# A two-layer recurrence: the projections into PSUM spread over all steps, and the forget gate moved to another bank

## Chip, core and metric

One of the eight cores of a Trainium2 chip runs the kernel. The metric is the time of one execution in microseconds (us); lower is better. Engines are named as in the profile: PE (TensorE matmuls), PEld (TensorE weight loads), DVE (VectorE), ACT (ScalarE), POOL (GpSimd), SP (the queue that issues most DMAs).

## What is computed

N = 32 sequences of T = 128 steps with 128 features pass through two recurrent layers, each with a residual.

```python
def _L0_cond_ref(x, h0, Wx, Wh, b):          # layer 0, an LSTM
    xW = jnp.einsum('ntd,dg->ntg', x, Wx) + b
    def step(carry, xw_t):
        prev_h, prev_c = carry
        a = xw_t + prev_h @ Wh
        i = jax.nn.sigmoid(a[:, :Hdim])
        f = jax.nn.sigmoid(a[:, Hdim:2 * Hdim])
        o = jax.nn.sigmoid(a[:, 2 * Hdim:3 * Hdim])
        g = jnp.tanh(a[:, 3 * Hdim:])
        next_c = f * prev_c + i * g
        next_h = o * jnp.tanh(next_c)
        return ((next_h, next_c), next_h)
...
def _L1_cond_ref(x, h0, weight, bias):       # layer 1, a UGRNN
    def step(h, xt):
        m = jnp.concatenate([xt, h], axis=-1) @ weight + bias
        c = jnp.tanh(m[:, units:])
        g = jax.nn.sigmoid(m[:, :units] + 1.0)
        h_new = g * h + (1.0 - g) * c
        return (h_new, h_new)
...
x = x + _L0_cond_ref(x, cond_1024, L0_cond_Wx, L0_cond_Wh, L0_cond_b)
x = x + _L1_cond_ref(x, cond_1024, L1_cond_weight, L1_cond_bias)
```

## The kernel before

Everything lies transposed: features on the 128 partitions, the 32 sequences in the free dimension. Each engine runs its own program, a body of 16 steps (`BODY`) that is written out in full: once for the first 16 steps, six times as a hardware loop, once for the last 16. Inside a body `j` is the step, `m = j // 8` the half and `k = j % 8` the place in the half. Semaphores with the step as their count order the engines; nothing is scheduled automatically, so the order in the code is the order on each engine.

A step of layer 0 goes round a loop. PE adds `Wh` times the state to the four gate sums in PSUM: the forget gate by an fp32 matmul on `hT` (`forget_sum`, L253), the others by three bf16 matmuls on `h_high` (`high`, L259) and one fp16 matmul on `h_low` (`low`, L263). Before, `high` of i and of g come first, then `low` of i and of g, then o. ACT applies the activations, always in the order forget, i, g, o (`gates`, L436). DVE multiplies the forget gate by the old cell (`keep`, L533), makes the new cell by a scan over pairs (`scan`, L539, once into the PSUM bank `cell_bank` for ACT and once into SBUF as `cell_kept`), ACT takes its tanh (L453), and DVE makes `hT`, `h_high` and `h_low` from it (L546, L547, L553). The forget gate is written into `act_bank` at columns 0 to 31, next to the tanh of the cell at 32 to 63. Since `h_high` of the step before reads that bank, ACT waits for `high_ready` as well as for `f_summed` ahead of the forget gate.

Layer 1 runs one step behind: 8 matmuls on `h_high` and `h_low` (`layer1_input`, L271 and L273), 12 on three parts of its own state (L279: `acts`, `u_rest`, `u_low`), two tanh on ACT (L458, L459), and on DVE `pair`, the state, `u_rest`, `u_low` and the two residual sums `x1T` and `outT` (L560 to L593). On DVE these are placed between `h_high` and `scan`, and `u_low` (L577) stands between `keep` and `scan`.

The input parts, x times the input weights plus bias, don't depend on the state. They are put into PSUM ahead, each gate's bank for 8 steps at a time: `project0` issues an fp32 matmul pair of 256 columns and a bias matmul of 256 columns at the end of the step before the bank's first one. `BEGIN = (3, 4, 5, 6)` gives the place at which the banks of f, i, g and o begin, so these land at the end of the steps k = 2, 3, 4 and 5. Layer 1's part takes a 256-column pair at k = 6 and at k = 7 (`project1`, L237) and a bias matmul of 512 columns at k = 0 (`bias1`, L242). At k = 1 nothing is projected. At k = 2 of the first half the PE waits on four semaphores (three x chunks and `f_ready`) ahead of the projection.

Ahead of step 0, 11 dummy matmuls (`WARM`) run while weights and x are being loaded; then come the first projections and `first_state` of i, g and o (there is no old cell in step 0), and layer 1's first projection.

Of the kernel before, what the change touches and what calls it, by code (L numbers as in the profile page):

```python
# [10 lines left out]
P = 128  # L11
N = 32
T = 128
GS = 8
HS = 4
# [14 lines left out]
BEGIN = (3, 4, 5, 6)  # L30
# [7 lines left out]
WARM = 11  # L38


def two_layer_recurrence(nc, xt, h_first, wx, wh, b, w1, out_t):
# [5 lines left out]
    with ctx:  # L47
# [136 lines left out]
        def _(sp):  # L184
# [40 lines left out]
        def _(pe):  # L225
            def project0(q, first, steps=GS):

                k = (first - BEGIN[q]) % GS
                to = gate_banks[q][:, k * N:(k + steps) * N]
                nc.tensor.matmul(to, wx_s[:, q * P:(q + 1) * P], xT[:, first * N:(first + steps) * N],  # L230
                                 start=True, stop=False, skip_group_check=True)
                nc.tensor.matmul(to, bias_lhs[:, :], pick[:, q:q + 1].to_broadcast([P, steps * N]),
                                 start=False, stop=False, skip_group_check=True)

            def project1(q, c, first):
                weights = w1x_gate[:, :] if q == 0 else w1_raw[:, 0, P:2 * P]
                return nc.tensor.matmul(a1[c][:, :].rearrange("p (t g n) -> p t g n", t=GS, g=2)[:, :, q, :], weights,  # L237
                                        xT[:, first * N:(first + GS) * N].rearrange("p (t n) -> p t n", t=GS),
                                        start=q == 0, stop=False, skip_group_check=True)

            def bias1(c):
                nc.tensor.matmul(a1[c][:, :].rearrange("p (t g n) -> p t g n", t=GS, g=2), bias_lhs[:, :],  # L242
                                 pick[:, NG:NG + 2].unsqueeze(1).unsqueeze(3).to_broadcast([P, GS, 2, N]),
                                 start=False, stop=False, skip_group_check=True)
# [62 lines left out]
            for _ in range(WARM):  # L307
                nc.tensor.matmul(a1[1][:, 0:2 * P], idle[:, 0:P], idle[:, :], start=True, stop=True,
                                 skip_group_check=True)

            pe.wait_ge(x_in[0], 16)
# [8 lines left out]
            project0(GATE_G, 0, BEGIN[GATE_G])  # L320
            first_state(GATE_G, g_summed)
            project0(GATE_O, 0, BEGIN[GATE_O])
            first_state(GATE_O, o_summed)

            project0(GATE_F, 1, BEGIN[GATE_F] - 1)
            pe.wait_ge(w1_gate_ready, 1)
            project1(0, 0, 0)
            bias1(0)

            def body(s0, first, last):  # L330
                for j in range(BODY):
                    s, m, k = s0 + j, j // GS, j % GS
                    r, l = s - 1, (j - 1) % BODY
                    if not (first and j == 0):
# [6 lines left out]
                        high(GATE_G, j)  # L341
# [3 lines left out]
                        low(GATE_I, j, i_summed)  # L345
                        low(GATE_G, j, g_summed)
                        high(GATE_O, j)
                        low(GATE_O, j, o_summed)
                        if first and j == 1:
                            project1(1, 0, 0)  # L350
# [5 lines left out]
                        else:  # L356
                            if first and j == 2:
                                pe.wait_ge(w1_cast, 4)
                                pe.wait_ge(w1_split, 4)

                            pe.wait_ge(acts1_ready, s - 1)
# [4 lines left out]
                        if k == 0:  # L366
                            bias1(m)

                    ends = last and m == 1
                    steps = BODY - 1 - j if ends else GS  # L370
                    if k == BEGIN[GATE_F] - 1:
# [317 lines left out]
```

## Time and profile before

| | |
|---|---|
| median of 3 runs | 246.23 us (245.77 to 249.11) |
| the profiled execution, its own time | 246.65 us |
| its span from first to last instruction | 244.9 us |
| PE busy | 227.5 us (93%) |
| DVE busy | 219.7 us (90%) |
| ACT busy | 117.8 us (48%) |
| granted TensorE clock, mean | 0.931 of full speed |

The span has 128 steps in it, each of which depends on the one before, so the time is a start, 127 step lengths, and an end. The share of an engine's busy time says little here, since matmuls overlap; the spacing of the steps says more. The profiled execution took 1.75 us more than its span, and 0.42 us more than the median.

### The profile page before, as it was taken

The page shows a single profiled execution, that of the slowest core. Times are in us where ns is not written, and L with a number is a line of the kernel's source. Part 1 is how long each engine was busy: PE and PEld are TensorE (multiplying, and loading weights), DVE is VectorE, ACT ScalarE, POOL GpSimd, SP SyncE. Part 2 cuts the span into 40 slices and gives each one's busy share as a digit, 9 for nine tenths or more (in the row PEclk, how much of TensorE's full clock was granted, in tenths as well). Part 3 has the DMA queues.
Part 4 walks back from the last instruction along what each step waited for, and adds up shares of the span by engine and source line. Part 5 has one row for each costly group of instructions (what it writes and reads, how often), then busy time and mean ns, then how long its engine had stood idle before and what let it go on. Part 6 is the DMA issues. An engine that isn't in the chain of part 4 may idle for free.

```text
span 244.9 us, 12629 instructions
## 1 busy us (share of the span) xinstructions
PE 227.5 (93%) x4631; PEld 193.3 (79%) x4631; DVE 219.7 (90%) x1557; ACT 117.8 (48%) x906; POOL 4.0 (2%) x12
## 2 busy tenths in 40 slices
PE   6999898999989899998989989898999989899993
PEld 4888787878878787887878778787878878787882
DVE  6669999999988989999997989999999999979884
ACT  3445455554544445454553544545554554545441
POOL 1400000000000000000000000000000000000000
PEclk9999999999989979999997979999999999979655
DMA  6000001000010000100010000100001000000000
GB/s 184 12 4 25 24 23 37 25 25 19 19 43 11 21 21 21 32 21 21 11 43 21 11 21 21 32 21 21 21 22 31 21 21 21 12 15 13 15 13 11
DMA packets 11969, 6.20 MB, mean 25 GB/s; under 512 B 1446, under 2 KB 11692, under 8 KB 11948
## 3 DMA queue, kind: packets, MB, share of 16 engines
q1 hardware_dynamic: 11792, 5.66, 8.1%
q8 instruction: 13, 0.21, 0.4%
q10 hardware_dynamic: 156, 0.27, 0.3%
q14 instruction: 8, 0.07, 0.1%
HBM read 3.82 MB, written 2.10 MB: 24 GB/s over the span
## 4 chain that ended last, share of the span: by engine, by line
DVE 61%; PE 21%; ACT 9%; issue 5%; DMA 1%; SPq 0%; ACTq 0%
DVE cell_bank L539 11%; ACT act_bank L453 8%; DVE hT L546 8%; DVE u_low L577 7%; DVE pair L560 6%; DVE u_rest L572 5%; DVE acts L566 5%; PE gate_f L253 4%; DVE x1T L585 4%; DVE h_high L547 4%; PE gate_f L230 4%; DVE outT L593 4%; DVE h_low L553 4%; PE a L279 3%; DVE scan_add L533 3%
## 5 line engine op out<-in xcount | busy, mean ns | idle before, releaser
L253 PEld LDWEIGHTS gate_f<-hT,wh_raw 128*128 128x128 f32 x254 | 42.1, 207 | 38.4 <-DVE hT L546 34.5
L436 ACT ACTIVATE act_bank<-gate_f 128x32 f32<-128x32 f32 x127 | 23.1, 182 | 79.6 <-PE gate_f L253 79.6
L253 PE MATMUL gate_f<-hT,wh_raw 128*128 128x32 f32 x254 | 51.1, 285 | 10.7 <-DVE hT L546 10.7
L271 PE MATMUL a<-h_high,w1x_part 128*128 128x32 f16 x768 | 42.1, 178 | 0.9 <-DVE h_low L553 0.9
L453 ACT ACTIVATE act_bank<-cell_bank 128x32 f32<-128x32 f32 x128 | 23.3, 182 | 36.7 <-DVE cell_bank L539 36.6
L539 DVE TENSOR_TENSOR_SCAN cell_bank<-scan_mul,scan_add 128x64 f32<-128x64 f32 x128 | 38.6, 301 | 1.1 <-ACT scan_add L436 1.1
L279 PE MATMUL a<-acts,w1h_part 128*128 128x32 bf16 x762 | 38.6, 178 | 0.0
L273 PE MATMUL a<-h_low,w1x_fp 128*128 128x32 f16 x256 | 35.7, 178 | 0.0
L539 DVE TENSOR_TENSOR_SCAN cell_kept<-scan_mul,scan_add 128x64 f32<-128x64 f32 x128 | 34.2, 267 | 0.0
L546 DVE TENSOR_TENSOR hT<-out_gate,act_bank 128x32 f32<-128x32 f32 x128 | 23.8, 186 | 10.5 <-ACT act_bank L453 1.2
L271 PEld LDWEIGHTS a<-h_high,w1x_part 128*128 128x128 bf16 x768 | 31.9, 97 | 1.3 <-ACT acts L459 0.9
L259 PEld LDWEIGHTS gate_i<-h_high,wh_part 128*128 128x128 bf16 x381 | 32.3, 132 | 0.0
L279 PE MATMUL a<-u_rest,w1h_part 128*128 128x32 bf16 x508 | 32.2, 178 | 0.0
L533 DVE TENSOR_TENSOR scan_add<-act_bank,cell_kept 128x32 f32<-128x32 f32 x127 | 24.3, 191 | 7.7 <-ACT act_bank L436 7.2
L560 DVE SCALAR_TENSOR_TENSOR pair<-acts 128x64 f32<-128x64 f32 x128 | 28.7, 224 | 1.4 <-ACT acts L459 1.4
L259 PE MATMUL gate_i<-h_high,wh_part 128*128 128x32 f16 x381 | 29.9, 180 | 0.0
L458 ACT ACTIVATE acts<-a 128x64 f32<-128x64 f32 x128 | 28.1, 219 | 1.9 <-PE a L279 1.5
L259 PE MATMUL gate_g<-h_high,wh_part 128*128 128x32 f16 x381 | 29.0, 178 | 0.0
L259 PE MATMUL gate_o<-h_high,wh_part 128*128 128x32 f16 x381 | 29.0, 178 | 0.0
L279 PEld LDWEIGHTS a<-acts,w1h_part 128*128 128x128 bf16 x762 | 28.3, 97 | 0.0
L279 PE MATMUL a<-u_low,w1h_part 128*128 128x32 bf16 x254 | 27.6, 185 | 0.0
L436 ACT ACTIVATE out_gate<-gate_o 128x32 f32<-128x32 f32 x128 | 26.3, 205 | 1.1 <-PE gate_o L248 1.1
(97 smaller groups left out, 612.8 us busy)
## 6 DMA issues: line engine op xcount, KB each, us to landing
xT<-in_x_dram SPq DMA_DIRECT2D x46, 64.0 KB, 1.8
out_dram<-outT SPq DMA_DIRECT2D x32, 64.0 KB, 1.6
wx_s<-in_L_cond_Wx_dram SPq DMA_DIRECT2D x1, 256.0 KB, 2.7
wh_raw<-in_L_cond_Wh_dram ACTq DMA_DIRECT2D x1, 256.0 KB, 2.9
w_raw<-in_L_cond_weight_dram SPq DMA_DIRECT2D x1, 256.0 KB, 3.5
bias_rows<-in_biases_dram ACTq DMA_DIRECT2D x1, 3.0 KB
condT<-in_cond_dram SPq DMA_DIRECT2D x1, 16.0 KB, 2.5
```

Of the source, the lines that this page charges most:

```text
L253: nc.tensor.matmul(gate_step(GATE_F, j), wh_raw[:, GATE_F * P:(GATE_F + 1) * P], hT[:, (j - 1) % RING, :], start=False, stop=True, skip_gr ...
L259: nc.tensor.matmul(gate_step(q, j), wh_part[:, w, (q - 1) * P:q * P], h_high[:, (j - 1) % PARTS, :], start=False, stop=False, skip_group_c ...
L271: nc.tensor.matmul(to, w1x_part[:, w, q * P:(q + 1) * P], h_high[:, j % PARTS, :], start=False, stop=False, skip_group_check=True)
L273: nc.tensor.matmul(to, w1x_fp16[:, q * P:(q + 1) * P], h_low[:, j % PARTS, :], start=False, stop=False, skip_group_check=True)
L279: mm = nc.tensor.matmul(a1_step(j)[:, q * N:(q + 1) * N], w1h_part[:, w, q * P:(q + 1) * P], moving, start=False, stop=parts == 1, skip_gr ...
L436: return nc.scalar.activation(out, gate_step(q, j), func)
L453: nc.scalar.activation(tanh_c[:, :], cell[:, :, 1], ACT.Tanh).then_inc(tanh_c_ready, 1)
L458: nc.scalar.activation(acts1[:, 0:4:3, i, :], a1_step(j).rearrange("p (g n) -> p g n", g=2), ACT.Tanh)
L533: nc.vector.tensor_tensor(scan_add[:, :, 1], forget[:, :], cell_kept[:, :, 1], ALU.mult).then_inc(scan_in_ready, 1)
L539: nc.vector.tensor_tensor_scan(to[:, :, :].rearrange("p n two -> p (n two)"), scan_mul[:, :, :].rearrange("p n two -> p (n two)"), scan_ad ...
L546: nc.vector.tensor_tensor(hT[:, j % RING, :], out_gate[:, :], tanh_c[:, :], ALU.mult).then_inc(h_ready, 1)
L560: nc.vector.scalar_tensor_tensor(out=pair1[:, :, :], in0=acts1[:, 0:2, i, :], scalar=1.0, in1=acts1[:, 2:4, i, :], op0=ALU.add, op1=ALU.mu ...
```

## The change

Six things are changed.

1. The banks begin at other places: `BEGIN = (7, 1, 3, 5)` for f, i, g, o. Each gate's bank is filled in halves over two steps: at the first (k = 0, 2, 4, 6 for i, g, o, f) an fp32 pair of 128 columns, which opens the bank, and the bias for all 8 steps; at the second (k = 1, 3, 5, 7) the other 128-column pair.
2. Layer 1's projection is made in quarters of 128 columns, at k = 1, 3, 5 and 7; its bias goes in halves of 256 columns to k = 2 and 6. So each step of the eight now ends in some projection. Each of the two steps that fill a bank has a wait of its own for the gate having been read.
3. In the last half body, where projections shrink or fall away, 2, 2, 4, 2 and 4 dummy matmuls of 256 columns are added at k = 1, 3, 5, 6 and 7.
4. `low` of gate i is issued right behind `high` of gate i, ahead of gate g.
5. The forget gate is written into `cell_bank` (columns 64 to 95), and ACT's wait for `high_ready` is gone.
6. At the start, x chunk 0 is loaded ahead of the first state and layer 1's weights ahead of x chunk 1; gates i, g, o, f are projected for 1, 3, 5 and 6 steps; i's and g's first states are both issued ahead of o's projection; layer 1's first projection has 128 columns, and the rest of it and its bias move into the steps 1 to 3. There are 12 dummy matmuls in place of 11.

The core of the diff:

```diff
-BEGIN = (3, 4, 5, 6)
+BEGIN = (7, 1, 3, 5)
-        forget, tanh_c = act_bank[:, 0:N], act_bank[:, N:2 * N]
+        forget, tanh_c = cell_bank[:, 2 * N:3 * N], act_bank[:, 0:N]
...
             sp.dma_start(wx_s[:, :], wx).then_inc(wx_in, 16)
+            load_x(0, 0)
             sp.dma_start(condT[:, :], h_first).then_inc(cond_in, 16)
-            load_x(0, 0)
+            sp.dma_start(w1_raw[:, :, :], w1.rearrange("(h k) n -> k h n", h=2)).then_inc(w1_in, 16)
             load_x(1, 1)
-            sp.dma_start(w1_raw[:, :, :], w1.rearrange("(h k) n -> k h n", h=2)).then_inc(w1_in, 16)
...
-            project0(GATE_I, 0, BEGIN[GATE_I])
+            project0(GATE_I, 0, 1)
+            bias0(GATE_I, 0, 1)
+            project0(GATE_G, 0, 3)
+            bias0(GATE_G, 0, 3)
             pe.wait_ge(wh_in, 16)
             pe.wait_ge(cond_in, 16)
             first_state(GATE_I, i_summed)
+            first_state(GATE_G, g_summed)
             pe.wait_ge(x_in[1], 16)
...
                         high(GATE_I, j)
-                        high(GATE_G, j)
...
                         low(GATE_I, j, i_summed)
+                        high(GATE_G, j)
                         low(GATE_G, j, g_summed)
...
-                    if k == BEGIN[GATE_I] - 1:
-                        pe.wait_ge(scan_in_ready, 2 * s + 1)
-                        project0(GATE_I, j + 1, steps)
...
+                    if k == 0:
+                        if m == 0:
+                            pe.wait_ge(x_in[0], s0 + 16)
+                            pe.wait_ge(x_in[1], s0 + 16)
                         pe.wait_ge(scan_in_ready, 2 * s + 1)
+                        project0(GATE_I, a, a_steps)
+                        bias0(GATE_I, a, BODY - a if ends else GS)
+                    if k == 1:
+                        if not ends:
+                            pe.wait_ge(x_in[2 if m == 0 else 4], s0 + 16)
+                        pe.wait_ge(scan_in_ready, 2 * s + 1)
+                        project0(GATE_I, b, b_steps, False)
+                        if not ends:
+                            project1(0, 1 - m, 0, next1)
+                        else:
+                            warm(0, 2)
...
-
-                    act.wait_ge(high_ready, s)
                     act.wait_ge(f_summed, s)
```

How this moves instructions is seen at three places. The first is PE in the loop body, from the end of step j = 1 of the first half (place k = 1) into the next step. `a_0` and `a_1` are layer 1's two banks. Before:

```order
L279 MATMUL a_0<-u_low,w1h_part 128x32 [waits u_low_ready]
L279 MATMUL a_0<-u_low,w1h_part 128x32
L335 REGISTER_ALU
L253 MATMUL gate_f<-hT,wh_raw 128x32 [waits h_ready]
L259 MATMUL gate_i<-h_high,wh_part 128x32 [waits high_ready]
L259 MATMUL gate_i<-h_high,wh_part 128x32 x2
L259 MATMUL gate_g<-h_high,wh_part 128x32 x3
L263 MATMUL gate_i<-h_low,wh_fp 128x32 [waits low_ready]
L263 MATMUL gate_g<-h_low,wh_fp 128x32
```

And in the changed kernel:

```order
L287 MATMUL a_0<-u_low,w1h_part 128x32 [waits u_low_ready]
L287 MATMUL a_0<-u_low,w1h_part 128x32
L400 ISA [waits x_in2]
L229 MATMUL gate_i<-xT,wx_s 128x128 [waits scan_in_ready]
L245 MATMUL a_1<-xT,w1x_gate 128x4x32
L349 REGISTER_ALU
L261 MATMUL gate_f<-hT,wh_raw 128x32 [waits h_ready]
L267 MATMUL gate_i<-h_high,wh_part 128x32 [waits high_ready]
L267 MATMUL gate_i<-h_high,wh_part 128x32 x2
L271 MATMUL gate_i<-h_low,wh_fp 128x32 [waits low_ready]
L267 MATMUL gate_g<-h_high,wh_part 128x32 x3
L271 MATMUL gate_g<-h_low,wh_fp 128x32
```

Two 128-column pairs and two waits have come between the last matmul of layer 1 and the forget sum, where there was nothing, and gate g's three `h_high` matmuls now stand behind gate i's last.

The second place is ACT, one regular step from the forget gate to the tanh of the cell. Before:

```order
L436 ACTIVATE act_bank<-gate_f 128x32 [waits f_summed,high_ready]
L436 ACTIVATE scan_mul<-gate_i 128x32 [waits i_summed]
L436 ACTIVATE scan_add<-gate_g 128x32 [waits g_summed]
L436 ACTIVATE out_gate<-gate_o 128x32 [waits o_summed]
L453 ACTIVATE act_bank<-cell_bank 128x32 [waits cell_ready]
```

And in the changed kernel:

```order
L491 ACTIVATE cell_bank<-gate_f 128x32 [waits f_summed]
L491 ACTIVATE scan_mul<-gate_i 128x32 [waits i_summed]
L491 ACTIVATE scan_add<-gate_g 128x32 [waits g_summed]
L491 ACTIVATE out_gate<-gate_o 128x32 [waits o_summed]
L506 ACTIVATE act_bank<-cell_bank 128x32 [waits cell_ready]
```

The order is the same; the forget gate has one wait in place of two and another bank as its target.

The third place is PE at the start, from the first projection to layer 1's. Before:

```order
L230 MATMUL gate_i<-xT,wx_s 128x128 [waits pick_ready,bias_ready,wx_in,x_in0]
L232 MATMUL gate_i<-pick,bias_lhs 128x128
L248 MATMUL gate_i<-condT,wh_raw 128x32 [waits cond_in,wh_in]
L230 MATMUL gate_g<-xT,wx_s 128x160 [waits x_in1]
L232 MATMUL gate_g<-pick,bias_lhs 128x160
L248 MATMUL gate_g<-condT,wh_raw 128x32
L230 MATMUL gate_o<-xT,wx_s 128x192
L232 MATMUL gate_o<-pick,bias_lhs 128x192
L248 MATMUL gate_o<-condT,wh_raw 128x32
L230 MATMUL gate_f<-xT,wx_s 128x64
L232 MATMUL gate_f<-pick,bias_lhs 128x64
L237 MATMUL a_0<-xT,w1x_gate 128x8x32 [waits w1_gate_ready]
```

And in the changed kernel:

```order
L229 MATMUL gate_i<-xT,wx_s 128x32 [waits pick_ready,bias_ready,wx_in,x_in0]
L235 MATMUL gate_i<-pick,bias_lhs 128x32
L229 MATMUL gate_g<-xT,wx_s 128x96
L235 MATMUL gate_g<-pick,bias_lhs 128x96
L256 MATMUL gate_i<-condT,wh_raw 128x32 [waits cond_in,wh_in]
L256 MATMUL gate_g<-condT,wh_raw 128x32
L229 MATMUL gate_o<-xT,wx_s 128x160 [waits x_in1]
L235 MATMUL gate_o<-pick,bias_lhs 128x160
L256 MATMUL gate_o<-condT,wh_raw 128x32
L229 MATMUL gate_f<-xT,wx_s 128x192
L235 MATMUL gate_f<-pick,bias_lhs 128x192
L245 MATMUL a_0<-xT,w1x_gate 128x4x32 [waits w1_gate_ready]
```

Gate g's projection now stands ahead of gate i's first state and no longer waits for x chunk 1. Behind these rows the bias of layer 1 (512 columns) stood before; now a projection of gate i with its bias stands there.

## Rows read from the trace of the kernel before

**Rows 1.** The page: busy time and share by engine, and the granted clock in 40 slices.
```profile
PE 227.5 (93%) x4631; PEld 193.3 (79%) x4631; DVE 219.7 (90%) x1557; ACT 117.8 (48%) x906; POOL 4.0 (2%) x12
PEclk9999999999989979999997979999999999979655
```

**Rows 2.** Stretches between starts of `hT`: length, DVE busy on L546 (count), clock, DMA.
```profile
17.33:240.03 222.70, 23.09 (x125) 0.94 0.08 22
45.21:67.75 22.54, 2.42 (x13) 1.00 0.08 23
39.86:67.75 27.89, 2.98 (x16) 1.00 0.09 26
67.75:97.75 30.00, 2.98 (x16) 0.89 0.08 22
211.23:240.03 28.80, 2.81 (x16) 0.74 0.05 14
```

**Rows 3.** Two pairs of steps: length, busy PE, PEld, DVE, ACT, POOL, clock, DMA.
```profile
67.75:71.22 3.47, 2.70 (x70) 2.48 (x70) 3.32 (x25) 1.77 (x16) 0.00 (x0) 1.00 0.16 46
71.22:76.02 4.80, 4.80 (x76) 4.03 (x77) 3.40 (x25) 1.79 (x16) 0.00 (x0) 0.64 0.10 27
```

**Rows 4.** One regular step in order of time: start, duration, engine, line, operation.
```profile
40.10 0.41 PE L253 MATMUL gate_f<-hT,wh_raw 128*128 128x32 f32 x2 [0.23 <-DVE hT L546]
40.22 0.18 DVE L553 SCALAR_TENSOR_TENSOR h_low<-hT,h_high 128x32 f16<-128x32 f32 x1
...
40.50 0.18 PE L263 MATMUL gate_i<-h_low,wh_fp 128*128 128x32 f16 x1
...
40.61 0.18 ACT L436 ACTIVATE act_bank<-gate_f 128x32 f32<-128x32 f32 x1 [0.56 <-PE gate_f L253]
...
40.67 0.18 DVE L593 SCALAR_TENSOR_TENSOR outT<-acts,x1T 128x32 f32<-128x32 f32 x1
...
40.81 0.19 ACT L436 ACTIVATE scan_add<-gate_g 128x32 f32<-128x32 f32 x1
40.82 0.19 DVE L533 TENSOR_TENSOR scan_add<-act_bank,cell_kept 128x32 f32<-128x32 f32 x1
...
40.93 0.18 DVE L577 TENSOR_TENSOR u_low<-u_rest 128x32 bf16<-128x32 f32 x1
...
41.05 0.30 DVE L539 TENSOR_TENSOR_SCAN cell_bank<-scan_mul,scan_add 128x64 f32<-128x64 f32 x1
...
41.17 0.21 PE L279 MATMUL a<-u_low,w1h_part 128*128 128x32 bf16 x2
...
41.38 0.18 ACT L453 ACTIVATE act_bank<-cell_bank 128x32 f32<-128x32 f32 x1 [0.29 <-DVE cell_bank L539]
...
41.84 0.30 PE L253 MATMUL gate_f<-hT,wh_raw 128*128 128x32 f32 x1 [0.45 <-DVE hT L546]
```

**Rows 5.** PE at the projection of gate f, k = 2, first half of a body, full clock.
```profile
42.90 0.21 PE L279 MATMUL a<-u_low,w1h_part 128*128 128x32 bf16 x2
43.21 0.67 PE L230 MATMUL gate_f<-xT,wx_s 128*128 128x256 f32 x2
```

**Rows 6.** The same place in the second half of the body, full clock.
```profile
56.92 0.22 PE L279 MATMUL a<-u_low,w1h_part 128*128 128x32 bf16 x2
57.03 0.67 PE L230 MATMUL gate_f<-xT,wx_s 128*128 128x256 f32 x2
57.53 0.27 PE L232 MATMUL gate_f<-pick,bias_lhs 128*128 128x256 bf16 x1
57.64 0.36 PE L253 MATMUL gate_f<-hT,wh_raw 128*128 128x32 f32 x2
```

**Rows 7.** PE in the start, before the first forget sum.
```profile
8.66 1.20 PE L237 MATMUL a<-xT,w1x_gate 128*128 128x256 f32 x2
9.65 0.63 PE L242 MATMUL a<-pick,bias_lhs 128*128 128x512 bf16 x1
10.08 0.47 PE L253 MATMUL gate_f<-hT,wh_raw 128*128 128x32 f32 x2
```

More of the change, by code:

```diff
@@ L225, in _, with project0 @@
         def _(pe):
-            def project0(q, first, steps=GS):
+            def project0(q, first, steps, begins=True):
                 k = (first - BEGIN[q]) % GS
[L229 to L232, printed above, removed]
+                nc.tensor.matmul(gate_banks[q][:, k * N:(k + steps) * N], wx_s[:, q * P:(q + 1) * P],
+                                 xT[:, first * N:(first + steps) * N], start=begins, stop=False,
+                                 skip_group_check=True)
@@ L233, in project0, with bias0, half1 @@
+            def bias0(q, first, steps=GS):
+                k = (first - BEGIN[q]) % GS
+                nc.tensor.matmul(gate_banks[q][:, k * N:(k + steps) * N], bias_lhs[:, :],
+                                 pick[:, q:q + 1].to_broadcast([P, steps * N]),
                                  start=False, stop=False, skip_group_check=True)
-            def project1(q, c, first):
+            def half1(c, half):
+                return a1[c][:, half * GS * N:(half + 1) * GS * N].rearrange("p (t g n) -> p t g n", t=HS, g=2)
@@ L236, in project1 @@
+            def project1(q, c, half, first):
                 weights = w1x_gate[:, :] if q == 0 else w1_raw[:, 0, P:2 * P]
[L237 to L243, printed above, removed]
+                return nc.tensor.matmul(half1(c, half)[:, :, q, :], weights,
+                                        xT[:, first * N:(first + HS) * N].rearrange("p (t n) -> p t n", t=HS),
+                                        start=q == 0 and half == 0, stop=False, skip_group_check=True)
@@ L244, in bias1 @@
+            def bias1(c, half):
+                nc.tensor.matmul(half1(c, half), bias_lhs[:, :],
+                                 pick[:, NG:NG + 2].unsqueeze(1).unsqueeze(3).to_broadcast([P, HS, 2, N]),
                                  start=False, stop=False, skip_group_check=True)
@@ L306, in _, with warm @@
             idle = ident[:, :].bitcast(BF16)
-            for _ in range(WARM):
-                nc.tensor.matmul(a1[1][:, 0:2 * P], idle[:, 0:P], idle[:, :], start=True, stop=True,
-                                 skip_group_check=True)
+            def warm(c, times):
+                for _ in range(times):
+                    nc.tensor.matmul(a1[c][:, 0:2 * P], idle[:, 0:P], idle[:, :], start=True, stop=True,
+                                     skip_group_check=True)
+            warm(1, WARM)
             pe.wait_ge(x_in[0], 16)
@@ L356, in body @@
                         else:
+                            pe.wait_ge(acts1_ready, s - 1)
                             if first and j == 2:
+                                project1(0, 0, 1, HS)
+                                bias1(0, 1)
                                 pe.wait_ge(w1_cast, 4)
                                 pe.wait_ge(w1_split, 4)
-                            pe.wait_ge(acts1_ready, s - 1)
+                            if first and j == 3:
+                                project1(1, 0, 1, HS)
                             layer1_input(l)
```

77 lines of the change are left out of this document (50 added, 27 removed).

## The prediction

> **What bounds the kernel now.** I read the page first, then stretches cut at the starts of `hT`, then one regular step. On the page PE and DVE are both busy nearly all the time, which decides nothing, but the clock row is not even: it dips in several slices and is low for the whole end [rows 1]. The stretches turn this into step lengths. Undisturbed, 13 steps take 22.54 us, 1.734 each; a whole body of 16 steps at full clock takes 27.89, which is 16 x 1.734 = 27.74 and 0.15 more; the body at 67.75 takes 30.00 at 0.89 of the clock, and the last 15 steps 28.80 at 0.74 [rows 2]. From 17.33 to 240.03 there are 124 step lengths in 222.70 us, where 124 x 1.734 would be 215.0 [rows 2]. So 7.7 us of the span are steps longer than the regular one. Ahead lie the start (17.3 us, three long steps in it), behind the end (4.9 us).
>
> What makes the regular step 1.734 us is seen in its rows [rows 4]. The forget sum ends at 40.10 + 0.41 = 40.51, ACT starts the forget gate at 40.61, `keep` starts at 40.82, `u_low` 0.11 later, the scan at 41.05, the tanh at 41.38, and the next forget sum starts at 41.84. DVE is nearly full, but one of its starts waits: `outT` starts at 40.67 and `keep` 0.15 later, where `u_low` follows `keep` after 0.11 and `scan` follows `u_low` after 0.12. `keep` waits for the forget gate, which ends at 40.79. PE has room: between layer 1's last matmuls (41.17) and the next forget sum (41.84) lie 0.67 us [rows 4].
>
> What makes the long steps is PE's clock. At the steps k = 0 and 1, PE does little besides the recurrence: busy 2.70 of 3.47 us at full clock. The two steps behind them, which carry the large projections, then took 4.80 us at a mean clock of 0.64 [rows 3], where two regular ones take 3.47. PE's clock has fallen from 2.4 to 1.2 GHz for most of them, and at half rate a projection no longer fits into the 0.67 us.
>
> **Part 1, the projections spread out.** The same columns are projected in the loop, so the sum of PE's work stays; each step now carries two 128-column pairs, or one pair and 256 to 512 bias columns. What it removes is the pair of light steps. Of the 7.7 us, 7 bodies have the 0.15 at k = 2 (1.05 us, below), and the rest, 6.7, goes with the low clock: the body at 67.75 has 30.00 - 27.89 = 2.1 more than an undisturbed one, the body at 125.64 nearly the same (29.82 us long, 1.9), and the last 15 steps have 28.80 - 26.01 - 0.15 = 2.6 [rows 2]. Every fall of the clock in the trace stands at or just behind a pair k = 0, 1; with no light pair left I take it that the clock stays at 2.4 GHz from the third or fourth step on. The last eight steps would be light, and there the added dummy matmuls stand for the missing projections. The gain is 6.7 us; the bounds are 0 (the clock falls as often as before) and 6.7.
>
> Does a step's projection fit into the gap? A 256-column pair and its bias matmul take from 57.03 to 57.64, 0.61 us, and start 0.11 behind layer 1's last matmuls; the forget sum then starts 0.72 after them in place of 0.67 [rows 6], and the step lengths there stay regular. A 128-column pair lies between a 32-column pair (the forget sum itself, at most 0.41) and the 256-column one (0.50 to its bias matmul [rows 6]); by its columns it takes 0.25 to 0.30. Two pairs take 0.5 to 0.6, a pair with 512 bias columns 0.5: inside. The 0.15 at k = 2 of the first half: there the projection starts 0.31 behind layer 1's last matmuls [rows 5], in the second half 0.11 [rows 6]. Four semaphores are waited for in the one, two in the other. In the changed kernel no place has four; k = 0 has three, with a pair and 256 bias columns behind (0.31 + 0.30 + 0.11 = 0.72, just inside), k = 1 two, with two pairs (0.2 + 0.6 = 0.8 at worst, 0.1 late in 8 steps). I take the 1.05 us as gained and up to 0.8 as a risk.
>
> **Part 2, the forget gate.** ACT starts the tanh 0.03 behind the end of the scan (41.05 + 0.30 = 41.35, start 41.38), but the forget gate 0.10 behind its sum (40.51, start 40.61) [rows 4]. The forget gate waits for two semaphores, and `high_ready` is long there; I read the 0.06 to 0.07 as the second wait being taken up only after the first. With one wait the gate starts at about 40.55 and ends at 40.73, `keep` could start at 40.76, and DVE itself is free for it at 40.67 + 0.11 = 40.78. So `keep` gains 0.037. The other bank costs nothing: ACT and DVE touch `cell_bank` at other times. The stall goes to DVE's own order; next late is gate g.
>
> **Part 3, gate i first.** `low` of i needs `h_low`, which ends at 40.22 + 0.18 = 40.40; PE starts its matmuls 0.06 behind a DVE result (`u_low` ends at 41.11, start 41.17), so i's `low` can start between 40.46 and 40.48 (now 40.50). Three matmuls of g and its `low` follow at 0.025 each (23 matmuls lie between 40.50 and 41.17, at most 0.029 each, and the last waits), so g's sum ends at up to 40.58 + 0.18 = 40.76. ACT takes g at 40.79 where it now does at 40.81, it ends at 40.99, and the scan can start at 41.02 in place of 41.05 [rows 4]. So of the 0.037 that part 2 gives, 0.027 arrive. Over 124 steps: 3.3 us. The bounds are 0 (the two waits cost nothing, or g comes as late as now) and 4.6 (all of 0.037). I take 3.3, since each latency in it has a row of the same step.
>
> **Part 4, the start.** The first projections are narrower and layer 1's is smaller ahead of the first forget sum. The clock is low here, though the page's row doesn't show it: a 256-column pair takes 0.99 us, twice the 0.50 of later, and 512 bias columns take 0.43, with the forget sum behind them at 10.08 [rows 6, 7]. Ahead of the first `hT`, gates i, g and o lose 96 + 64 + 32 columns, 0.0039 each (0.99 / 256), 0.7 us, and a DMA is moved ahead. But what is taken out comes back between the recurrence's own matmuls: counted up to the forget sum of step 3, PE has 64 projection columns more (0.25 us) and 448 bias columns more (0.38), in four more pairs, since the new banks open earlier. The first `hT` is then 0.6 earlier, and the fourth about 0.7 later if the clock rises where it does now, or 0.7 earlier if the denser work makes it rise sooner. I take 0 with bounds of -0.8 and +0.8. The end stays: it is a chain of DVE and ACT with a store.
>
> **The sum.** Against the profiled execution: 244.9 - 6.7 - 1.05 - 3.3 + 0 = 233.9 us of span, plus the 1.75 around it: 235.6 us. That execution was 0.42 above the median of 246.23, so the ratio is about 0.956.
>
> **The rule that speaks against it.** As the trace has it, PE had no gap of its own in the pair of steps before the fall: 2.70 of 3.47 us busy [rows 3], as in the same steps of bodies in which the clock stayed. The Trainium skill, "TensorE: Matmul & The Clock Gate", section "Why this matters for your kernels", asks for no idle gaps between bursts of matmuls to keep the fast clock; by that rule alone there is nothing here for spreading to remove, and the time would be that of the rival "clock not in our hands" below. Its section "A second HAM failure mode" tells of an oscillation by small idles between groups, which is nearer to what these rows show.
>
> **Rivals.**
> 1. *The step doesn't shorten.* The scan comes no earlier, since gate g's sum comes later by the three matmuls put ahead of it, or the second wait costs nothing. For: g is behind i by four matmuls now; against: the 0.10 and the 0.03 in one step. Then 235.6 + 3.3 = 238.9.
> 2. *The clock still falls at some places.* In the last eight steps the projections with their dummies are lighter than in the loop (at k = 3 and 4 above all), and the start is another phase. A pair of steps at low clock cost 4.80 - 3.47 = 1.3 with the large projections [rows 3]; one to three of them give 237 to 239.5.
> 3. *The clock is not in our hands.* The falls have another cause than the light pairs, and come as before: 235.6 + 6.7 = 242.3. Against: all stand behind the same pair.
> 4. *PE sets the step, and the kernel is slower.* A fp32 pair could cost by instruction and not by column: then a 128-column pair takes the 0.50 of the 256-column one, two of them with the lead of 0.11 take 1.11, against 0.72 that fits. Four of eight steps (k = 1, 3, 5, 7), 60 in all, would be 0.39 longer: 235.6 + 23 = 259. It decides from 0.61 for the two pairs. Against: 256 columns at low clock take twice the time at full clock (0.99 and 0.50 [rows 6, 7]), so columns count.
>
> **How the numbers follow.** Forecast 0.62 (233 to 238), rival 1 0.16, rival 2 0.14, rival 3 0.05, rival 4 0.03. The low end is 235.6 - 1.3 (all of 0.037) - 0.8 (start) - 0.7: 232.8; the high end takes in rivals 1 and 2 and a start 0.8 longer: 240.0. Outside stay rivals 3 and 4 and edges of the rest. Two per cent, about what a measurement of this kernel can tell from no change, is at 241.3: faster 0.91, same 0.06, slower 0.03.
>
> **What would show it.** Right: a clock of 1.00 in every body and to the end; 16 steps in 27.3 us; the forget gate 0.03 to 0.04 behind its sum; `keep` 0.11 to 0.12 behind `outT`; no longer step at k = 2. Wrong: stretches of 0.5 clock in the loop (rivals 2, 3), a step of still 1.73 with gate g's activation ending later (rival 1), the forget sum idle-free behind the projections (rival 4), a fourth `hT` later than 18 us (part 4).

## The result, and the profile after

The changed kernel takes 234.18 us (median of 4 runs, 234.11 to 234.33), the kernel before beside it 247.3 us (245.77 to 249.11, 4 runs; one more than in the table ahead). The ratio is 0.947, with a 95% interval of 0.939 to 0.954. The profiled executions took 234.23 us (span 232.7) and 246.65 us (span 244.9), so 12.4 us are to be placed.

The page of the changed kernel, its busy times and its clock row; they answer to [rows 1].
```profile
PE 226.2 (97%) x4850; PEld 202.6 (87%) x4850; DVE 216.3 (93%) x1557; ACT 124.8 (54%) x906; POOL 4.0 (2%) x12
PEclk9999999999999999999999999999999999999999
```
The dips and the low end are gone. (The row reads 9 in the start too, where the matmuls run at half speed, as is seen below.) PE's busy time hardly changes (227.5 to 226.2 us), though it has 219 more matmuls to do.

Stretches between starts of `hT` (now L599), with the columns of [rows 2]: from the fifth `hT` to the last, the bodies from 37.67 and from 65.08, and the last 15 steps. The counts take in the instruction at either edge.
```profile
17.12:227.77 210.65, 23.25 (x124) 1.00 0.08 23
37.67:65.08 27.41, 3.02 (x17) 1.00 0.10 26
65.08:92.48 27.40, 3.02 (x17) 1.00 0.08 24
202.08:227.77 25.69, 2.84 (x16) 1.00 0.06 16
```
123 steps in 210.65 us are 1.7126 each, and all of them lie between 1.711 and 1.715: every body is 16 times that. In the trace the low clock is found before 10.13 us and after 232.0 only.

All engines in the pairs k = 0, 1 and k = 2, 3 of the body at 65.08, the columns of [rows 3].
```profile
65.08:68.50 3.42, 3.42 (x78) 3.24 (x79) 3.27 (x24) 1.88 (x16) 0.00 (x0) 1.00 0.16 46
68.50:71.93 3.43, 3.43 (x79) 3.09 (x76) 3.28 (x25) 1.89 (x16) 0.00 (x0) 1.00 0.06 19
```
PE is busy 3.42 us of the pair that had 2.70 of 3.47 before [rows 3]; the four steps are alike.

One regular step of the changed kernel in order of time, as in [rows 4].
```profile
39.76 0.28 PE L261 MATMUL gate_f<-hT,wh_raw 128*128 128x32 f32 x1
39.99 0.19 PE L271 MATMUL gate_i<-h_low,wh_fp 128*128 128x32 f16 x1
40.03 0.23 PE L267 MATMUL gate_g<-h_high,wh_part 128*128 128x32 f16 x3
40.08 0.18 ACT L491 ACTIVATE cell_bank<-gate_f 128x32 f32<-128x32 f32 x1 [0.50 <-PE gate_f L261]
40.11 0.18 PE L271 MATMUL gate_g<-h_low,wh_fp 128*128 128x32 f16 x1
...
40.20 0.18 DVE L646 SCALAR_TENSOR_TENSOR outT<-acts,x1T 128x32 f32<-128x32 f32 x1
...
40.30 0.18 DVE L586 TENSOR_TENSOR scan_add<-cell_bank,cell_kept 128x32 f32<-128x32 f32 x1
...
40.32 0.20 ACT L491 ACTIVATE scan_add<-gate_g 128x32 f32<-128x32 f32 x1
...
40.41 0.18 DVE L630 TENSOR_TENSOR u_low<-u_rest 128x32 bf16<-128x32 f32 x1
...
40.55 0.30 DVE L592 TENSOR_TENSOR_SCAN cell_bank<-scan_mul,scan_add 128x64 f32<-128x64 f32 x1
```
The forget gate starts 0.04 us behind its sum (39.76 + 0.28 = 40.04, start 40.08), where it was 0.10 [rows 4]. `keep` follows `outT` after 0.10 and not 0.15, `u_low` follows `keep` after 0.11. The wait stands in another place now: the scan starts 0.14 behind `u_low`, and 0.03 behind the end of gate g's activation (40.32 + 0.20 = 40.52).

PE at a step that has two projection pairs, k = 3. [rows 5, 6] show a projection in the kernel before.
```profile
42.40 0.20 PE L287 MATMUL a<-u_low,w1h_part 128*128 128x32 bf16 x2
42.45 0.48 PE L229 MATMUL gate_g<-xT,wx_s 128*128 128x128 f32 x2
42.76 0.39 PE L245 MATMUL a<-xT,w1x_gate 128*128 128x128 f32 x2
43.06 0.30 PE L261 MATMUL gate_f<-hT,wh_raw 128*128 128x32 f32 x1
```
The first pair starts 0.05 us behind the first of layer 1's last two matmuls, the second 0.31 behind the first, and the forget sum at its usual place: two pairs fit, and no step is longer at k = 2 or anywhere else.

PE in the start, which answers to [rows 7].
```profile
2.77 1.49 PE L318 MATMUL a<-ident 128*128 128x256 bf16 x6
4.05 0.61 PE L229 MATMUL gate_i<-xT,wx_s 128*128 128x32 f32 x2
...
8.08 0.69 PE L245 MATMUL a<-xT,w1x_gate 128*128 128x128 f32 x2
8.56 0.63 PE L229 MATMUL gate_i<-xT,wx_s 128*128 128x128 f32 x2
8.99 0.42 PE L235 MATMUL gate_i<-pick,bias_lhs 128*128 128x256 bf16 x1
9.20 0.47 PE L261 MATMUL gate_f<-hT,wh_raw 128*128 128x32 f32 x2
...
10.28 0.27 PE L250 MATMUL a<-pick,bias_lhs 128*128 128x256 bf16 x1
```
The same 256 bias columns take 0.42 us at 8.99 and 0.27 at 10.28: the clock has gone from 1.2 to 2.4 GHz between them. The clock events of the trace put the rise at 10.13 us, before at 16.67. And the first forget sum starts 0.88 us earlier (9.20 for 10.08 [rows 7]). The first five `hT` start at 8.08, 11.07, 13.26, 15.15 and 17.12 us; before at 9.06, 12.05, 14.75, 17.33 and 19.06. Of the 1.94 us at the fifth, 0.98 are there at the first, with the clock low in both kernels; the rest comes in the four steps behind it, in which the clock rises.

So the 12.4 us are: the bumps at k = 2 1.05; the regular step 1.7335 to 1.7126, 0.021 x 123 = 2.6; the start up to the fifth `hT` 1.94; and the low clock in the loop 6.7, which is what remains of the 10.3 us between the fifth and the last `hT`. The end stays at 4.9, and 0.15 lie outside the span.

### The profile page after: what moved, and what is told of

Its sections match the earlier page's. It is cut to its first block, busy times and chain, and to the rows that moved or that the text cites. A ratio compares the mean times of both kernels' runs of the same rounds, so it can differ in the third digit from the quotient of the medians.

```text
span 232.7 us, 12952 instructions
## 1 busy us (share of the span) xinstructions
PE 226.2 (97%) x4850; PEld 202.6 (87%) x4850; DVE 216.3 (93%) x1557; ACT 124.8 (54%) x906; POOL 4.0 (2%) x12
## 4 chain that ended last, share of the span: by engine, by line
DVE 78%; ACT 10%; PE 6%; issue 4%; POOL 0%; ACTq 0%; POOLq 0%
DVE cell_bank L592 15%; ACT act_bank L506 10%; DVE hT L599 10%; DVE u_low L630 9%; DVE pair L613 9%; DVE u_rest L625 7%; DVE acts L619 6%; DVE x1T L638 6%; DVE h_low L606 5%; DVE h_high L600 5%; DVE outT L646 5%; DVE scan_add L586 1%; PE a L318 1%; PE a L245 1%; PE a L287 1%
## 5 line engine op out<-in xcount | busy, mean ns | idle before, releaser
L491 ACT ACTIVATE cell_bank<-gate_f 128x32 f32<-128x32 f32 x127 | 23.1, 182 | 63.6 <-PE gate_f L261 63.6
L261 PEld LDWEIGHTS gate_f<-hT,wh_raw 128*128 128x128 f32 x254 | 38.0, 189 | 21.3 <-DVE hT L599 14.8
L599 DVE TENSOR_TENSOR hT<-out_gate,act_bank 128x32 f32<-128x32 f32 x128 | 24.2, 189 | 10.4 <-ACT act_bank L506 1.1
L267 PEld LDWEIGHTS gate_i<-h_high,wh_part 128*128 128x128 bf16 x381 | 30.1, 125 | 0.0
L267 PE MATMUL gate_i<-h_high,wh_part 128*128 128x32 f16 x381 | 29.3, 178 | 0.0
L491 ACT ACTIVATE scan_mul<-gate_i 128x32 f32<-128x32 f32 x128 | 25.7, 201 | 1.0 <-PE gate_i L256 0.8
L512 ACT ACTIVATE acts<-a 128x32 f32<-128x32 f32 x128 | 26.0, 203 | 0.0
L491 ACT ACTIVATE scan_add<-gate_g 128x32 f32<-128x32 f32 x128 | 25.8, 202 | 0.2 <-PE gate_g L256 0.2
```

Of the source, the lines that this page charges most:

```text
L261: nc.tensor.matmul(gate_step(GATE_F, j), wh_raw[:, GATE_F * P:(GATE_F + 1) * P], hT[:, (j - 1) % RING, :], start=False, stop=True, skip_gr ...
L267: nc.tensor.matmul(gate_step(q, j), wh_part[:, w, (q - 1) * P:q * P], h_high[:, (j - 1) % PARTS, :], start=False, stop=False, skip_group_c ...
L491: return nc.scalar.activation(out, gate_step(q, j), func)
L512: nc.scalar.activation(acts1[:, 1, i, :], a1_step(j)[:, 0:N], ACT.Tanh, scale=-1.0).then_inc(acts1_ready, 1)
L599: nc.vector.tensor_tensor(hT[:, j % RING, :], out_gate[:, :], tanh_c[:, :], ALU.mult).then_inc(h_ready, 1)
```

## The experiments

Twelve kernels, in three groups of four, each group timed beside the kernel before (medians of 245.72, 247.38 and 246.98 us). Times are medians of 4 runs. Where kernels of different groups are set beside each other, the step lengths in their traces say more than the medians. No kernel leaves out a part of the reference's computation; where dummies change, they are matmuls whose result nothing reads.

**Is it the second wait or the bank, and what does the order bring?** In the changed kernel:
```
a2   if not first:
+        act.wait_ge(high_ready, s)
         act.wait_ge(f_summed, s)
a1   high(GATE_I, j)
+    high(GATE_G, j)
     ...
     low(GATE_I, j, i_summed)
-    high(GATE_G, j)
c2   both
```
The second wait back:

> The changed kernel with ACT's wait for high_ready put back ahead of the forget gate, which still goes to cell_bank. The semaphore is long there, so only the taking up of a second wait is added. If that costs 0.06 us per step at the forget gate (my theory), the gate starts 0.10 behind its sum, keep 0.15 behind outT, the step is 1.73 and the time about 237. If the bank is what helps, the step stays 1.713 and the time 234.2.

The order back:

> The changed kernel with gate g's three h_high matmuls put back ahead of gate i's last matmul. If gate g's sum sets the scan (my theory), undoing it makes i come later and g follow it on ACT by 0.09: a step of 1.71 to 1.72 us, a time of 234.2 to 235.2. If the order is what shortens the step at all, the step is 1.73 and the time 236.5 to 237. If the order only delays g, the step is 1.70 and the time 232 to 232.8.

Both back, which leaves the spread projections and the new start:

> The changed kernel with both of its step edits undone (ScalarE's second wait and the order of the kernel before); its spread projections, its start and its dummies at the end stay. Theory, the step is then the one of before and the parts add up: a step of 1.7335 us, no clock falls before the end, no bump at k = 2; a fifth hT at 16.5 to 17.3 us, 123 steps and 4.9 us of end give a span of 234.6 to 235.5 us, total 236.4 to 237.3 us; ratio 0.955 to 0.965. Rival, the spread projections themselves lengthen or shorten the step (their places differ per step): a step off 1.7335 us by over 0.005, or unequal steps.

237.21 us (ratio 0.970, 0.963 to 0.976), 235.45 us (0.960, 0.957 to 0.963) and 236.81 us (0.961, 0.958 to 0.965). A body at full clock of each, with the columns of [rows 2] but all of DVE as the engine: with the wait back,
```profile
65.25:93.03 27.78, 26.61 (x192) 1.00 0.08 24
```
with the order back,
```profile
64.62:92.22 27.60, 26.43 (x192) 1.00 0.08 24
```
and with both back.
```profile
64.90:92.67 27.77, 26.60 (x192) 1.00 0.08 24
```
The steps are 1.736, 1.725 and 1.736 us, beside 1.7125 with neither. With the wait back, and with both back, the theories held; with the order back the step (forecast 1.71 to 1.72) and the time (up to 235.2) lie just above their theory's range. The new order brings nothing while there are two waits, and 0.0125 with one; taking the wait away brings 0.011 in the old order and 0.0235 in the new one. So each of two things sets the scan once the other is out of the way. The rows with the wait back:
```profile
48.14 0.41 PE L261 MATMUL gate_f<-hT,wh_raw 128*128 128x32 f32 x2
...
48.64 0.18 ACT L491 ACTIVATE cell_bank<-gate_f 128x32 f32<-128x32 f32 x1 [0.56 <-PE gate_f L261]
...
48.83 0.20 ACT L491 ACTIVATE scan_add<-gate_g 128x32 f32<-128x32 f32 x1
48.85 0.19 DVE L587 TENSOR_TENSOR scan_add<-cell_bank,cell_kept 128x32 f32<-128x32 f32 x1
```
and with the order back.
```profile
48.32 0.20 ACT L491 ACTIVATE scan_add<-gate_g 128x32 f32<-128x32 f32 x1
48.40 0.18 DVE L630 TENSOR_TENSOR u_low<-u_rest 128x32 bf16<-128x32 f32 x1
...
48.55 0.30 DVE L592 TENSOR_TENSOR_SCAN cell_bank<-scan_mul,scan_add 128x64 f32<-128x64 f32 x1
```
With two waits, in the cell's bank, the forget gate is again 0.09 behind its sum (48.14 + 0.41 = 48.55, start 48.64), and `keep` starts 0.03 behind the gate's end (48.82): the wait costs it, not the bank. With one wait and the old order, the scan follows 0.03 behind the end of gate g's activation (48.52): g's sum is next late. With both back the step is 1.736 for 1.7335, so the spread projections leave it as it was, to 0.003 us.

The same in the kernel before, where only the bank and the wait are changed:

> Of the whole change the kernel before gets the forget gate's move alone: it lies in the cell's bank and ScalarE waits for f's sum only. The profiled run with the second wait put back in the changed kernel had steps of 1.736 us, against 1.7125 us. If the wait alone is what those 0.023 us are, they need both parts here too: with g's high products still ahead of i's low ones, the run with the order put back gave 1.725 us. So here a regular step of 1.722 to 1.728 instead of 1.7335, which is 0.7 to 1.4 us of 124 steps; the bumps at k = 2 and the clock's falls stay as before, so 243.5 to 245.5 us in all, ratio 0.990 to 0.998. Rival, the path runs through the scan's other operand even in this order: a step of 1.733 and a ratio of 1.000. Rival, the wait is worth the same wherever the order stands: 1.710 and a ratio of 0.988.

241.29 us (0.976, 0.965 to 0.988), a step of 1.7225. A body at full clock, with its bump of 1.838 at k = 2, all of DVE:
```profile
98.64:126.31 27.67, 26.49 (x193) 1.00 0.08 24
```
The step is the first theory's. The total fell by 6 us, and not by the 0.7 to 1.4 of the expectation: the step gives 0.011 x 124 = 1.4, and the bump at k = 2 is smaller (1.830 to 1.838 us for 1.887, 0.3 in all). The rest goes with the clock. Its mean over an execution is 0.944, 0.962, 0.965 and 0.971 here, and 0.918 to 0.947 in the seven of the kernel before beside them. The trace is that of the longest of the four (245.19 us; the others took 239.3 to 242.0); the clock falls four times in its loop, where the trace of before has five falls. Why there are fewer falls with a step 0.011 us shorter stays open.

**Are the light steps what brings the clock down?** In the kernel before:
```
a4  +if k == 1:
    +    for _ in range(4):
    +        nc.tensor.matmul(a1[1 - m][:, 0:2 * P], idle[:, 0:P], idle[:, :], start=True, stop=True,
    +                         skip_group_check=True)
```


> The kernel before with four dummy matmuls of 256 columns at the end of each step k = 1 (which has no projection), nothing moved. If the light pair k = 0, 1 brings the clock down (my theory), no fall is left up to the last body, the bodies at 67.75 and 125.64 take 27.9 us, and the time is 4 us under that of before, about 242; the end stays low. If the falls have another cause, the time is that of before, 246 to 248.

239.88 us (0.977, 0.969 to 0.984). The clock row, and PE in a pair k = 0, 1 and in a body:
```profile
PEclk9999999999999999999999999999999999999995
```
```profile
66.85:70.32 3.47, 3.14 (x74) 1.00 0.16 46
...
38.92:66.85 27.93, 27.37 (x587) 1.00 0.09 26
```
Work that nothing needs, four matmuls of 256 columns in eight steps, takes the clock's falls away: PE is busy 3.14 of the pair's 3.47 us where it was 2.70 [rows 3], and the clock stays up until 232.6 us. Nothing else was moved, and the mean clock is 0.984 to 0.990 in all four executions, 0.911 to 0.951 in the seven of before. The expectation had the end staying low and 242 us; the last body has these dummies too, and its clock stayed up. The bump of 0.15 stays in six bodies; in the last it is 0.06.

In the changed kernel, without its dummies in the last eight steps:

> The changed kernel without the dummy matmuls of the last half body. If light steps bring the clock down (my theory), it is at 0.5 in part of the last eight steps and the time is 0.5 to 2 us longer, 234.7 to 236.2. If the falls have another cause, nothing changes: 234.2.

234.0 us (0.953, 0.950 to 0.956), where the changed kernel, in another group, took 234.18. The clock did fall without the dummies, at 225.43 us and so 2.7 us ahead of the last `hT` (mean clock 0.980 to 0.984 in all four executions, 0.997 to 0.999 with them), but one step of 1.911 us is all that came of it; the expectation of 0.5 to 2 us was too high.

**Is the bump at k = 2 four waits in a row?** In the kernel before:
```
b4  +if k == 1 and m == 0:
    +    pe.wait_ge(x_in[0], s0 + 16)
    +    pe.wait_ge(x_in[1], s0 + 16)
     if k == BEGIN[GATE_F] - 1:
    -    for chunk in (range(3) if m == 0 else range(4, 5)):
    +    for chunk in (range(2, 3) if m == 0 else range(4, 5)):
```


> The kernel before, where at k = 2 of a body's first half PE waits for three chunks of x ahead of gate f's projection; here two of the three waits stand at k = 1 and one stays. If the three waits in a row make the step of 1.887 us in each body (0.154 us over the regular one), it goes and each body that has a full clock lasts 27.74 us instead of 27.89: 7 x 0.15 = 1.05 us less, ratio 0.995 to 0.996. If the bump is gate f's projection landing in that step, it stays at 27.89 and the ratio is 1.000. If the waits only move, the bump comes at k = 1 instead and the body stays 27.89 us.

243.41 us (0.986, 0.976 to 0.996). A body at full clock, all of DVE:
```profile
40.70:68.44 27.74, 26.58 (x192) 1.00 0.10 27
```
27.74 for 27.89 [rows 2], and all sixteen steps between 1.733 and 1.738: the waits made the bump. At k = 1 of the loop's bodies the two that were moved cost nothing that the step lengths show; no projection stands behind them there. In the last body a step there is 1.797, 0.06 longer, which a4 has at k = 2. The total fell by 4 us, where the expectation had 1.05 (a ratio of 0.995 to 0.996); as with b1, the mean clock was higher than beside it (0.943 to 0.958 for 0.918 to 0.947), and why stays open.

**What made the start shorter?** In the changed kernel, the old order of the loads (`condT`, chunk 0, chunk 1, `w1_raw`), once with 11 dummies and once with 16:
```
b2   sp.dma_start(wx_s[:, :], wx).then_inc(wx_in, 16)
    -load_x(0, 0)
     sp.dma_start(condT[:, :], h_first).then_inc(cond_in, 16)
    +load_x(0, 0)
    +load_x(1, 1)
     sp.dma_start(w1_raw[:, :, :], ...).then_inc(w1_in, 16)
    -load_x(1, 1)
    -WARM = 12
    +WARM = 11        (c1: 16)
```


> The changed kernel with the loads issued in the order of before (h_first ahead of the first chunk, w1 behind the second) and 11 dummies instead of 12; its shorter first projections stay. The changed kernel's first five hT start at 8.08, 11.07, 13.26, 15.15 and 17.12 us and its clock rises at 10.13 us; before they start 0.98 us later at the first and 1.94 us later at the fifth, and the clock rises at 16.67 us. If the load order makes the difference, the first hT goes back by about 1 us and the total by 1 to 2 us, to 235.2 to 236.2 us. If the shorter projections in front of the first state make it (their PE time is on the path, at a clock of 1.2 GHz), the first hT stays within 0.3 us of 8.08 and the total at 234.0 to 234.6 us. The steps stay at 1.7125 us in both.

> The kernel with the old order of loads (235.5 us; x's first chunk arrives 0.74 us after the last of 11 dummies, the clock rises at 15.9 us, first hT at 8.84, fifth at 19.48 us), now with 16 dummies, which last until about 4.93 us. If TensorE's idle gap between the dummies and the first projection is what put off the clock's rise, the gap is gone and the clock rises between 4.5 and 11 us: the fifth hT at 17.0 to 18.0 us, total 233.9 to 234.7 us. Rival, only the late arrival of the chunk counts: fifth hT at 19.4 to 19.6 us and 235.3 to 235.8 us in all, as with 11 dummies.

235.54 us with 11 (0.954, 0.944 to 0.965; runs from 234.5 to 236.5) and 233.53 us with 16 (0.947, 0.944 to 0.951). PE's start with 11 dummies:
```profile
2.77 1.27 PE L318 MATMUL a<-ident 128*128 128x256 bf16 x5
4.79 0.63 PE L229 MATMUL gate_i<-xT,wx_s 128*128 128x32 f32 x2 [0.74 <-DMA xT<-in_x_dram]
...
14.68 0.42 PE L250 MATMUL a<-pick,bias_lhs 128*128 128x256 bf16 x1
```
and with 16.
```profile
2.77 2.34 PE L318 MATMUL a<-ident 128*128 128x256 bf16 x10
4.91 0.48 PE L229 MATMUL gate_i<-xT,wx_s 128*128 128x32 f32 x2
...
7.77 0.27 PE L235 MATMUL gate_i<-pick,bias_lhs 128*128 128x256 bf16 x1
```
With 11, PE is idle 0.74 us in front of its first projection; 256 bias columns still take 0.42 us at 14.68, the clock rises at 15.9 us, and the fifth `hT` starts at 19.48, as before (19.06), though the narrow projections are there. With 16 the first projection starts later still, at 4.91, but without a gap: the same columns take 0.27 us at 7.77, the clock rises at 5.67 us, and the fifth `hT` starts at 16.58, which is earlier than its theory had it (17.0 to 18.0). So the late load costs its time only where PE goes idle over it. The five dummies close the gap and are more work at once; the two are not told apart. Of all fourteen traces, the nine without a gap in front of the first projection have the clock up from between 4.2 and 5.7 us on (six of them) or from 10.1 to 10.4 us (three), the five with one (0.54 to 1.47 us) from between 10.8 and 21.3 us on, the earliest of them with a gap of 0.85. What decides between the early and the late ones of a kind stays open. The Trainium skill, "TensorE: Matmul & The Clock Gate", section "Why this matters for your kernels", asks for TensorE to be kept busy continuously to get its full clock; here, in the start, the trace agrees (a gap of 0.74 us and the rise at 15.9, none and the rise at 5.67).

**Can gate g come earlier still?** In the changed kernel one (b3) or two (c3) of g's three high products stand ahead of i's `low`:
```
b3   high(GATE_I, j)
    +high(GATE_G, j, range(1))            (c3: range(2))
     ...
     low(GATE_I, j, i_summed)
    -high(GATE_G, j)
    +high(GATE_G, j, range(1, 3))         (c3: range(2, 3))
```


> The changed kernel with the first of gate g's three high products issued ahead of gate i's low ones, and two behind them. Of the changed kernel's step i's sum is done 0.10 us ahead of g's, and ScalarE does i first anyway; with all three of g's ahead the step is 1.725 us. If PE only fills a gap there (it waits for u's low half at that place), the first product costs i's sum nothing and brings g's sum forward by one matmul of about 0.025 us: a step of 1.69 to 1.705 us, 1 to 2.5 us less in all, 231.7 to 233.2 us. If PE is never idle between them, i comes later by as much as g is earlier by nothing: 1.7125 us or up to 1.717 us, 234.2 to 234.8 us.

> With one of gate g's high products ahead of i's low one the step is 1.700 us; here two are ahead. In that trace TensorE has a gap of one product's time (0.604 minus 0.567 us, against 0.025 us of one) in front of i's low product, and one after it; ScalarE works i, g, o at 0.094 and 0.082 us behind one another, i first. Theory, i's sum now sets ScalarE's chain: a second product ahead moves i's low product by 0.01 to 0.025 us, so the step is 1.708 to 1.725 us, 233.0 to 235.0 us in all. Rival, g's sum still sets it: the step falls by another 0.013 us to 1.687, 230.4 us in all.

232.02 us with one (0.942, 0.933 to 0.951) and 232.37 us with two (0.942, 0.938 to 0.946); the step is 1.700 in both. PE and ACT with one ahead:
```profile
47.56 0.18 PE L267 MATMUL gate_g<-h_high,wh_part 128*128 128x32 f16 x1
47.60 0.19 PE L271 MATMUL gate_i<-h_low,wh_fp 128*128 128x32 f16 x1
...
47.83 0.20 ACT L492 ACTIVATE scan_mul<-gate_i 128x32 f32<-128x32 f32 x1
...
47.92 0.20 ACT L492 ACTIVATE scan_add<-gate_g 128x32 f32<-128x32 f32 x1
```
and with two.
```profile
48.22 0.18 PE L271 MATMUL gate_i<-h_low,wh_fp 128*128 128x32 f16 x1
...
48.44 0.20 ACT L492 ACTIVATE scan_mul<-gate_i 128x32 f32<-128x32 f32 x1
...
48.53 0.20 ACT L492 ACTIVATE scan_add<-gate_g 128x32 f32<-128x32 f32 x1
```
One product ahead is free: PE waits for `h_low` there. The second brought neither what its theory said nor its rival: i's `low` starts 0.013 later but takes 0.177 in place of 0.189 us, so its sum is done at the same 0.79 us behind `hT`, ACT starts i at 0.83 and g 0.094 behind it in both. (The profile models the ends of matmuls; that ACT starts at the same time is measured.) From here on, by these rows, gate i's sum and ACT's spacing set the scan; the row of g's sum (done 0.03 us earlier with two) has no say.

**Does it take the spread projections at all?** The kernel before with five small edits: the dummies of a4, the bank and the wait of b1, the waits of b4, the order of b3, and the changed kernel's order of loads with 12 dummies (all shown above).

> The kernel before with its projections where they were, and five small edits: four dummies of 256 columns at each k = 1 (239.9 us), forget gate beside the cell with one wait, one of g's high products ahead of i's low ones, two of the x waits at k = 1, the new order of loads with 12 dummies. If the parts add up whatever carries them: the clock up throughout, a step of 1.700 us, bodies of 27.2 us without a bump, fifth hT at about 17.5 us, 232.0 to 233.5 us in all. Rival, the lumps of projection (512 columns in one step) meet the shorter step: a bump of 0.05 us or more at k = 2, 3, 4 or 5 of each half, 16 x 0.05 to 0.15 = 0.8 to 2.4 us more, 233.5 to 236 us.

232.37 us (0.944, 0.940 to 0.949). PE from the fifth `hT` to the last, and in one body:
```profile
16.60:225.74 209.14, 204.07 (x4503) 1.00 0.08 24
64.21:91.41 27.20, 26.68 (x586) 1.00 0.08 24
```
16 steps in 27.20 us, without a bump: the parts add up, whatever carries them. The start too: with the wide first projections of before, its fifth `hT` starts at 16.60, as with the narrow ones and 16 dummies (16.58; the clock rises at 5.05 and 5.67), so the loads and the dummies make the start, and the narrow projections are not needed for it. This kernel is as fast as the one with spread projections and the same order (232.02), and both are faster than the changed kernel (234.18, in another group) by some 2 us, 0.0125 x 123 = 1.5 of it by the step.

## Why the prediction was right, and where not

The forecast was 235.6 us and a ratio of 0.956, measured were 234.2 and 0.947. Point by point:

**Clock and spreading (part 1): right in mechanism and size.** 6.7 us of falls are gone. That light steps bring the clock down was an inference from where the falls stood; dummies at k = 1 alone showed it. The objection that PE had "no gap of its own" there was read too coarsely: in such a pair PE is idle in spells of 0.23 and 0.45 us [rows 4], none in the loop is longer than 0.45, and bodies with a fall and without one have the same. The dummies fill the spell of 0.45 and add work at once, and the falls are gone; the two are not told apart. A 128-column pair was put at 0.25 to 0.30 us and takes 0.31 from its start to the next one's. The 1.05 us of the bumps is right to 0.1 (the last body's is 0.06, where it can be seen), and so is the cause, with the waits split. The 0.8 us of risk at k = 1 did not come. That the last eight steps need their dummies was so for the clock and not for the time.

**Forget gate (part 2): right.** The gate starts 0.04 behind its sum, `keep` 0.10 behind `outT` (forecast 0.11 to 0.12).

**Gate i first (part 3): right mechanism, 0.7 us too large.** The forecast was 0.027 us of a step and 3.3 in all, measured were 0.021 and 2.6. Counted from `hT`, i's `low` starts at 0.604 us (forecast 0.60 to 0.62), g's at 0.718 (0.72), ACT's g at 0.931 (0.93), the scan at 1.165 (1.16, by the forecast 0.03 less than before, where the unrounded trace has 1.187). So the step "the scan can start at 41.02 in place of 41.05" holds, and its difference of 0.03 (0.027 in the sum) was 0.022: the term was made of latencies read to 0.01 us, and 0.005 us of that times 124 steps is 0.6 us. The text took g's sum as the next late thing, and the order put back showed it; that one product could go ahead of i's `low` for nothing stood in the same rows and was not seen.

**The start (part 4): wrong.** "I take 0 with bounds of -0.8 and +0.8" measured -1.94 us. The failed step is "a DMA is moved ahead", which was put down without a price. That the columns alone bring nothing by the fifth `hT` is right: with the old loads and 11 dummies it starts at 19.48 for 19.06. Their size was too large both ways: there the first `hT` is 0.22 earlier (forecast 0.6) and the fourth 0.20 later (forecast 0.7), with x arriving 0.2 later. What the sum left out is the gap: before, PE was idle for 0.54 us in front of its first projection. The move and the twelfth dummy close it, the first projection starts at 4.05 for 4.59, and the clock rises at 10.13 for 16.67; that such a gap goes with a late rise is what the fourteen traces show, and one pair of them (11 and 16 dummies) tests. The prediction had the other branch, "0.7 earlier if the denser work makes it rise sooner", but looked for its cause in the columns and not in the gap, and had it at a third of its size.

The two misses have opposite signs: 1.94 too little, 0.7 too much, and 0.15 outside the span make the 1.4 us. That the sum came so close is in part luck: without the 0.7 on the other side it would have been 2.1 us off.

## What to carry to other kernels

When the clock falls in a loop, look at the lightest stretch in front of the fall and not at the heavy one in which the time is lost; a few dummies there tell within one run whether spreading the work is worth its code, and here they were as good. Don't credit one trace's count of falls to an edit: two kernels whose edit was worth 1 to 1.7 us came out 4 to 6 us faster, the rest of it going with the clock. A start is priced with its gaps: when a load moves, ask which engine waits for it and what its clock does afterwards. And where an engine waits with an order of operands written out by hand, look for the product of the next sum that fits into the wait.

## What the runs showed of the hardware

- A second semaphore wait ahead of an activation costs 0.06 us although it was met before (with and without it the gate starts 0.097 and 0.037 us behind the sum's end); four waits ahead of a projection on PE made a step of the loop 0.15 us longer, and with two of them a step earlier it was not.
- PE's clock fell from 2.4 to 1.2 GHz five times in a loop in which PE is never idle for longer than 0.45 us, each time in or just behind two light steps (in the pair that was read, a matmul is in flight for 2.70 of 3.47 us); with dummies in the same steps (3.14 of 3.47 us) it did not fall.
- With an idle gap of 0.5 to 1.5 us in front of the first projection the clock rose at 10.8 to 21.3 us, without one at 4.2 to 10.4; five more dummies over the gap were worth 2 us (235.54 and 233.53).
- A matmul that has waited for its operand shows 0.189 us and, started 0.013 us later behind another matmul, 0.177; what waits for its sum (ACT, 0.83 us behind `hT`) starts at the same time in both.
